# Batch 1's down products moved from fp32 parts to half-precision parts

## The chip, the cores and the metric

The kernel runs on one core of one Trainium2 chip. The core has five engines that run their own instruction streams: TensorE (PE in the profile, with its weight loads as PEld), VectorE (DVE), ScalarE (ACT), GpSimd (POOL) and SyncE (SP, here a queue of DMA issues). They wait for each other by semaphores. The metric is the device time of one execution in microseconds (us); less is better.

## The reference, cut to what matters

Four batches of 512 rows by 512 columns go through an attention-like block and then a feed-forward block with a residual sum each:

```python
x = x + _L0_attn_ref(_layernorm(x), W_q, W_kv, W_o)
x = x + _L0_ffn_ref(_layernorm(x), gate_w, up_w, down_w, gate_scale, up_scale, down_scale)

# attention: per head of 32 columns
qf  = l2_normalize(fft(q));  kvf = cumsum(l2_normalize(fft(kv)), axis=1)
out = ifft(qf * kvf).real @ W_o.T

# feed-forward, weights rounded to fp8, I = 1536
gate = silu((x @ gate_w8) * gate_scale)
up   = (x @ up_w8) * up_scale
y    = ((gate * up) @ down_w8) * down_scale
```

The change touches only the last product, `(gate * up) @ down_w8`, and what feeds it.

## The kernel before

**Tiling.** A batch `b` (0 to 3) has four row tiles `t` of 128 rows. The feed-forward has 12 slices `i` of 128 inner columns; a slice's number over all batches is `n = 12 * b + i`. TensorE makes for each slice a gate product in the PSUM bank `bg` and an up product in `bu` (`pe_gate_up`, 8 matmuls of 128x512 each), and a down product `pe_down` (8 matmuls: four row tiles `t`, each with a high and a low part, added up over the 12 slices in the banks `bd0` to `bd3`).

**Between them, for slice n:** ScalarE makes `sl` = silu(`bg`) (`act_silu`), VectorE makes `ff` = `bu` * scale * `sl` (`dve_f`), ScalarE copies `ff` into the high part (`act_fu`), and VectorE subtracts it for the low part (`dve_fu`). `pe_down(n)` needs both. `ff`, `fu` and `sl` have two buffers each, by `n % 2`.

**Two forms of the down product.** For `n < HALF * NI` the two parts and the weights (`fu`, `dw`) are 32-bit floats (fp32r). From `n = HALF * NI` on they are 16-bit floats (`fu16`, `dw16`), which the profile names by the memory they borrow, `half` and `own`. GpSimd copies the weights to 16 bits (`pool_dw`, six copies). With 16 bits `ff` could overflow, so it is divided by a power of two, the unit, which is worked out from the data and multiplied back in at the end (`us2` takes the place of the up scales `us`, `ds2` that of the down scales `ds`). `HALF` is 2 before: batches 0 and 1 have the 32-bit form, batches 2 and 3 the 16-bit one.

**The unit** comes from the largest absolute weight of each part of `gu` (`dve_most`, six reductions of 128x2048), a few tiny steps (`dve_gus`), one tiny matmul with ones that adds over the partitions (`pe_bound`, two passes of 128x3), and a chain of tiny steps on the result (before: `act_bound`, then `dve_unit2`).

**Order.** Every engine's order is written out by hand. After batch 0's own section a loop `for b in 1..3` runs; its turn `b` begins with `pe_qk` of the batch `nxt = b + 1` (7 products of 12 matmuls), then the first gate and up product of batch `b`, the last down product of batch `b - 1`, the eighth `pe_qk`, and so on. In the same turn VectorE sums squares for `nxt` (`dve_sum`, eight of them), scales batch `b - 1`'s finished banks by `ds` (`dve_scale_out`, into `ff`, so it takes turns with `dve_f`), and GpSimd adds that to `h` (`pool_out`). `dve_f(b * NI + 1)` writes the `ff` buffer that the third `pool_out` reads, and so waits for it. Then comes `dve_norm_tail` of `nxt` (a reciprocal and three short steps), `dve_scale(nxt, 0, 1)`, ScalarE's `act_ks`, GpSimd's `pool_ks`, and with these TensorE's `pe_tri(nxt, 0)`.

**PSUM banks.** `ba0` and `ba1` pass from piece to piece in the order of `tenancies()`; a piece waits until its bank's last tenant has been read.

## Time and profile before

| what | value |
|---|---|
| median of 3 runs | 419.12 us (418.77 to 419.37) |
| the profiled execution | 419.79 us, of which 418.0 us from its first to its last instruction |
| busy | PE 408.8 us (98%), DVE 297.4 (71%), ACT 193.2 (46%), POOL 108.2 (26%) |
| mean granted TensorE clock | 0.996 of full speed |

Times in rows are microseconds from the start of the span. TensorE overlaps one matmul with the next: a 128x512 matmul is listed with 379 ns, and in a row of them one starts every 216 ns. The chain of waits follows the work that ended last back in time and shows what each piece added to it.

### The profile page before, as it was taken

Reading aid. Unit: us, or ns where it says so; the run is one execution under the profiler, and the core shown is the slowest. Engines: PE = TensorE matmul, PEld = TensorE weight load, DVE = VectorE, ACT = ScalarE, POOL = GpSimd, SP = SyncE. Lnnn points to the kernel's source line nnn. Section 1 sums busy time; section 2 is a strip of 40 time slices with the busy share of each in tenths; the row PEclk is TensorE's granted clock in tenths of the full one; section 3 lists DMA queues with packets and bytes.
Section 4 is the critical chain, followed back from the end, with each engine's and each line's share of the span. In section 5 each row is a group of like instructions: output and inputs, shape, how many; then the busy total and the mean of one; then the engine's idle time right before and its main releaser. Section 6 shows DMA issues by size and latency. Waiting matters only on the chain.

```text
span 418.0 us, 5504 instructions
## 1 busy us (share of the span) xinstructions
PE 408.8 (98%) x1897; PEld 202.8 (49%) x1897; DVE 297.4 (71%) x514; ACT 193.2 (46%) x323; POOL 108.2 (26%) x114
## 2 busy tenths in 40 slices
PE   7999999999999999999999999999999999999994
PEld 3744454445555554454555555454444444444442
DVE  4998998999999699997984972167865854422234
ACT  3687756587736245445242563255442441131220
POOL 0133551015154137043541012032461001300003
PEclk9999999999999999999999999999999999999998
DMA  8986546600181143232112014411112051200002
GB/s 249 264 267 239 163 117 162 149 17 2 38 256 36 26 77 71 57 127 74 28 26 50 2 29 101 72 50 53 26 26 52 0 77 25 100 2 0 2 0 101
DMA packets 57547, 33.55 MB, mean 80 GB/s; under 512 B 49456, under 2 KB 49840, under 8 KB 57392
## 3 DMA queue, kind: packets, MB, share of 16 engines
q1 hardware_dynamic: 57088, 32.93, 30.3%
q8 instruction: 15, 0.25, 0.3%
q10 hardware_dynamic: 432, 0.28, 0.2%
q14 instruction: 12, 0.10, 0.1%
HBM read 17.44 MB, written 4.19 MB: 52 GB/s over the span
## 4 chain that ended last, share of the span: by engine, by line
PE 89%; DMA 3%; DVE 3%; ACT 2%; POOL 1%; SPq 1%; issue 1%; POOLq 0%; DVEq 0%
PE bd L488 20%; PE bu L470 19%; PE bg L470 19%; PE ba L370 14%; PE ba L415 8%; PE bd L370 3%; DMA h<-x_dram 1%; PE ba L388 1%; PE bd L415 1%; DMA hT<-w_q_dram 1%; PE bd L388 1%; PE bd L356 1%; PE bu L415 1%; POOL xs L1603 1%; PE bg L447 0%
## 5 line engine op out<-in xcount | busy, mean ns | idle before, releaser
L470 PE MATMUL bu<-hT,gu 128*128 128x512 f16 x384 | 90.7, 379 | 0.0
L470 PE MATMUL bg<-hT,gu 128*128 128x512 f16 x376 | 89.0, 379 | 0.0
L1234 DVE SCALAR_TENSOR_TENSOR ff<-bu,us,sl 128x512 f32<-128x512 f32 x48 | 35.9, 748 | 56.0 <-PE bu L470 52.8
L741 ACT ACTIVATE sl<-bg,gs 128x512 f32<-128x512 f32 x48 | 32.9, 686 | 78.0 <-PE bg L470 77.0
L370 PE MATMUL ba<-wf,xT 128*128 128x512 f16 x288 | 63.2, 379 | 0.0
L470 PEld LDWEIGHTS bu<-hT,gu 128*128 128x128 f16 x384 | 37.5, 98 | 45.5 <-DVE ff L1234 0.6
L470 PEld LDWEIGHTS bg<-hT,gu 128*128 128x128 f16 x376 | 35.6, 98 | 44.9 <-issue 4.1
L488 PE MATMUL bd<-dw,fu 128*128 128x512 f32 x192 | 51.1, 411 | 0.0
L1634 POOL TENSOR_TENSOR h<-ff,h 128x512 f32<-128x512 f32 x14 | 17.5, 1272 | 122.2 <-DVE ff L1265 122.2
L370 PEld LDWEIGHTS ba<-wf,xT 128*128 128x128 f16 x288 | 27.9, 98 | 34.1 <-issue 1.1
L488 PE MATMUL bd<-own,half 128*128 128x512 f16 x184 | 43.0, 379 | 0.0
L1603 POOL TENSOR_TENSOR xs<-xn,xs 128x512 f16<-128x512 f32 x15 | 20.4, 1369 | 79.7 <-ACT xs L653 79.7
L488 PEld LDWEIGHTS bd<-dw,fu 128*128 128x128 f32 x192 | 36.1, 188 | 9.6 <-DVE fu L1241 0.4
L1616 POOL TENSOR_TENSOR ks<-qk,ks 128x512 f16<-128x512 f32 x16 | 21.2, 1325 | 48.8 <-ACT ks L704 48.8
L415 PE MATMUL ba<-wo,qk 128*128 128x512 f16 x144 | 32.6, 379 | 0.0
L1050 DVE TENSOR_REDUCE S<-tu 128x16 f32<-128x512 f32 x32 | 21.5, 676 | 11.2 <-ACT tu L667 11.2
L488 PEld LDWEIGHTS bd<-own,half 128*128 128x128 f16 x184 | 17.9, 98 | 21.9 <-DVE half L1241 0.6
L1241 DVE TENSOR_TENSOR half<-ff,half 128x512 f16<-128x512 f32 x23 | 19.3, 839 | 11.9 <-ACT half L747 11.7
L667 ACT ACTIVATE tu<-ba 128x512 f32<-128x512 f32 x24 | 14.3, 594 | 22.2 <-PE ba L370 22.2
L1139 DVE TENSOR_TENSOR qk<-qk,sc 128x512 f32<-128x512 f32 x32 | 23.0, 736 | 0.2
L1241 DVE TENSOR_TENSOR fu<-ff,fu 128x512 fp32r<-128x512 f32 x24 | 20.8, 872 | 3.2 <-ACT fu L747 3.0
L747 ACT ACTIVATE half<-ff 128x512 f16<-128x512 f32 x23 | 14.3, 623 | 18.4 <-PE bd L488 13.2
(201 smaller groups left out, 524.3 us busy)
## 6 DMA issues: line engine op xcount, KB each, us to landing
h<-x_dram SPq DMA_DIRECT2D x16, 256.0 KB, 4.2
out_dram<-h SPq DMA_DIRECT2D x15, 256.0 KB, 2.0
hT<-w_q_dram SPq DMA_DIRECT2D x4, 256.0 KB, 5.0
gu<-w_kv_dram SPq DMA_DIRECT2D x4, 256.0 KB, 4.4
hT<-gate_w_dram SPq DMA_DIRECT2D x2, 512.0 KB, 3.5
hT<-up_w_dram SPq DMA_DIRECT2D x2, 512.0 KB, 5.6
gu<-woT_dram SPq DMA_DIRECT2D x1, 1024.0 KB, 5.1
hT<-down_w_dram SPq DMA_DIRECT2D x2, 512.0 KB, 4.9
```

The lines of the kernel that those rows point to most:

```text
L370: m = e.matmul(ba[i][:, :], xT[:, b % 2, part_x, k, P * t:P * t + P], wf[:, w, part_w, k, :], start=k == 0 and part_x == part_w, stop=k == ...
L415: m = e.matmul(ba[i][:, :], src[:, part_p, P * j:P * j + P], wo[:, part_w, j, :], start=j == 0 and part_p == part_w, stop=j == KT - 1 and ...
L470: m = e.matmul(bk[:, :], gu[:, c, 4 * w + k, col:col + P], hT[:, b % 2, part, k, :], start=k == 0 and part == 0, stop=k == KT - 1 and part ...
L488: m = e.matmul(bd[t][:, :], fu_at(n)[:, part, P * t:P * t + P], (dw if n < HALF * NI else dw16)[:, i, :], start=i == 0 and part == 0, stop ...
L741: e.activation(sl[:, n % 2, :], bg[:, :], ACT.Silu, scale=gs[:, i:i + 1]).then_inc(a_silu, 1)
L1050: e.tensor_reduce(S[:, t, NH * w:NH * w + NH], v, AX.X, ALU.add).then_inc(v_sum, 1)
L1139: e.tensor_tensor(split_heads(qk[:, t, w, :]), split_heads(qk[:, t, w, :]), head_scale(t, w), ALU.mult).then_inc(v_kn if w else v_qn, 1)
L1234: e.scalar_tensor_tensor(out=ff[:, n % 2, :], in0=bu[:, :], scalar=(us if b < HALF else us2)[:, i:i + 1], in1=sl[:, n % 2, :], op0=ALU.mul ...
L1241: e.tensor_tensor(fu_at(n)[:, 1, :], ff[:, n % 2, :], high.bitcast(F32) if n < HALF * NI else high, ALU.subtract).then_inc(v_fu, 1)
L1603: e.tensor_tensor(xs[:, t % 2, 1, :], xn[:, t % 2, :], xs[:, t % 2, 0, :], ALU.subtract).then_inc(p_xl, 1)
L1616: e.tensor_tensor(ks[:, 1, t, :], qk[:, t, 1, :], ks[:, 0, t, :], ALU.subtract).then_inc(p_ks, 1)
L1634: e.tensor_tensor(hh, y_at(b, t), hh, ALU.add).then_inc(p_out, 1)
```

## The change

`HALF` becomes 1: batch 1's 12 down products take the 16-bit form as well. Its first scaling by the unit is then in `dve_f(12)`, the first of turn `b = 1`, so the unit has to be ready there. For this:

- the first of the six `dve_most` moves from the start of turn 1 back into batch 0's section, ahead of `dve_f(10)`;
- `pe_bound` moves from behind the eighth `pe_qk` into the middle of `pe_down(11)`;
- the tiny steps behind it move from turn 1's middle (behind `dve_fu(15)`) ahead of `dve_f(12)`; ScalarE's step goes, and the steps are other ones (seven on VectorE where there were one on ScalarE and six on VectorE); the scaling of `ds` stays where it was;
- `dve_sum(nxt, 2, 1)` moves ahead of these steps, and `dve_sum(nxt, 3, 1)` ahead of `dve_scale_out(b - 1, 2)`, both in turn 1 only;
- in turn 1 ScalarE's high part waits also until the last weight has been rounded.

```diff
-HALF = 2
+HALF = 1
...
-        order += [("qk", b, t, w) for t in (1, 2, 3) for w in range(2)]
-        if b == HALF:
+        order += [("qk", b, t, w) for t in (1, 2) for w in range(2)] + [("qk", b, 3, 0)]
+        if b == HALF + 1:
             order += [("bound",)]
+        order += [("qk", b, 3, 1)]
...
                 pe_gate_up(e, b, 0)
-                pe_down(e, b * NI - 1)
+                pe_down_tile(e, b - 1, NI - 1, 0)
+                pe_down_tile(e, b - 1, NI - 1, 1)
+                if b == HALF:
+                    pe_bound(e)
+                pe_down_tile(e, b - 1, NI - 1, 2)
+                pe_down_tile(e, b - 1, NI - 1, 3)
                 if nxt < NB:
                     pe_qk(e, nxt, 3, 1)
-                if nxt == HALF:
-                    pe_bound(e)
...
-        def act_bound(e):
-            e.wait_ge(s_bound, 1)
-            e.activation(bound[:, 3:6], ba[AT["bound",]][:, 0:3], ACT.Sqrt).then_inc(a_bound, 1)
...
         def dve_unit2(e):
-            e.wait_ge(a_bound, 1)
-            e.tensor_tensor(bound[:, 9:10], bound[:, 3:4], bound[:, 4:5], ALU.mult).then_inc(v_unit2, 1)
+            e.wait_ge(s_bound, 1)
+            e.tensor_copy(bound[:, 3:6], ba[AT["bound",]][:, 0:3]).then_inc(v_unit2, 1)
             e.wait_ge(v_unit2, 1)
...
+            e.tensor_scalar(bound[:, 9:10], bound[:, 3:4], bound[:, 4:5], 1e-30, ALU.mult, ALU.max).then_inc(v_unit2, 1)
+            e.tensor_scalar(bound[:, 10:11], bound[:, 5:6], 1e-30, None, ALU.max).then_inc(v_unit2, 1)
...
+            e.reciprocal(bound[:, 14:15], bound[:, 13:14]).then_inc(v_unit2, 1)
+            e.wait_ge(v_unit2, 6)
+            e.tensor_scalar(us2[:, :], us[:, :], bound[:, 14:15], None, ALU.mult).then_inc(v_unit2, 1)
...
             if n == HALF * NI:
-                e.wait_ge(v_unit2, 6)
+                e.wait_ge(v_unit2, 7)
...
+            dve_most(e, 0, 0)
             dve_f(e, 10)
...
-                if nxt == HALF:
+                if b == HALF:
                     dve_most(e, 2, 0)
                     dve_most(e, 2, 1)
                     dve_gus(e)
+                    dve_sum(e, nxt, 2, 1)
+                    dve_unit2(e)
                 dve_f(e, b * NI)
                 dve_scale_out(e, b - 1, 0)
                 dve_fu(e, b * NI)
-                if nxt < NB:
+                if b > HALF and nxt < NB:
                     dve_sum(e, nxt, 2, 1)
                 dve_scale_out(e, b - 1, 1)
                 if nxt < NB:
                     dve_sum(e, nxt, 3, 0)
+                    if b == HALF:
+                        dve_sum(e, nxt, 3, 1)
                 dve_scale_out(e, b - 1, 2)
                 dve_scale_out(e, b - 1, 3)
...
-                if nxt == HALF:
-                    dve_unit2(e)
+                if b == HALF:
+                    dve_unit_out(e)
```

TensorE before, in turn 1 from the first gate and up product on (`bd` and `fu` is the down product `pe_down(11)`, `ba0<-wf,xT` the eighth `pe_qk`, `bound` the tiny matmul):

```order
L470 MATMUL bu<-hT,gu 128x512 [waits dve_f]
L470 MATMUL bu<-hT,gu 128x512 x7
L488 MATMUL bd0<-dw,fu 128x512 [waits dve_rd,dve_fu]
L488 MATMUL bd0<-dw,fu 128x512
L488 MATMUL bd1<-dw,fu 128x512 x2
L488 MATMUL bd2<-dw,fu 128x512 x2
L488 MATMUL bd3<-dw,fu 128x512 x2
L370 MATMUL ba0<-wf,xT 128x512 [waits d_xT3,act_cp]
L370 MATMUL ba0<-wf,xT 128x512 x11
L377 MATMUL ba1<-bound,ones 128x3 [waits dve_most,act_cp]
L470 MATMUL bg<-hT,gu 128x512 [waits act_silu]
```

The same place on TensorE in the changed kernel:

```order
L471 MATMUL bu<-hT,gu 128x512 [waits dve_f]
L471 MATMUL bu<-hT,gu 128x512 x7
L489 MATMUL bd0<-dw,fu 128x512 [waits dve_rd,dve_fu]
L489 MATMUL bd0<-dw,fu 128x512
L489 MATMUL bd1<-dw,fu 128x512 x2
L378 MATMUL ba0<-bound,ones 128x3 [waits dve_most,act_cp]
L489 MATMUL bd2<-dw,fu 128x512 x2
L489 MATMUL bd3<-dw,fu 128x512 x2
L371 MATMUL ba1<-wf,xT 128x512 [waits d_xT3,act_cp]
L371 MATMUL ba1<-wf,xT 128x512 x11
L471 MATMUL bg<-hT,gu 128x512 [waits act_silu]
```

The tiny matmul now stands between the second and the third row tile of `pe_down(11)`, and the two `ba` banks have changed places.

VectorE before, from the last tiny step of `dve_gus` to the reciprocal of `dve_norm_tail` (`ff<-bu` is `dve_f`, `ff<-bd` is `dve_scale_out`, `fu<-ff` is `dve_fu`, `S<-tu` is `dve_sum`):

```order
L1092 TENSOR_TENSOR bound<-bound 128x3 [waits dve_most]
L1234 SCALAR_TENSOR_TENSOR ff<-bu,us,sl 128x512 [waits dve_fu,act_silu,pe_u]
L1265 TENSOR_TENSOR ff<-bd0,ds 128x512 [waits dve_fu,pe_d]
L1241 TENSOR_TENSOR fu<-ff,fu 128x512 [waits act_fu]
L1050 TENSOR_REDUCE S<-tu 128x16 [waits act_sq]
L1265 TENSOR_TENSOR ff<-bd1,ds 128x512 [waits dve_fu,pe_d]
L1050 TENSOR_REDUCE S<-tu 128x16 [waits act_sq]
L1265 TENSOR_TENSOR ff<-bd2,ds 128x512 [waits pool_out,pe_d]
L1265 TENSOR_TENSOR ff<-bd3,ds 128x512 [waits pool_out,pe_d]
L1050 TENSOR_REDUCE S<-tu 128x16 [waits act_sq]
L1234 SCALAR_TENSOR_TENSOR ff<-bu,us,sl 128x512 [waits dve_fu,pool_out,act_silu,pe_u]
L1119 RECIPROCAL y0<-Q 128x128 [waits act_rt1]
```

VectorE in the changed kernel, from the sum and the tiny steps that now stand ahead of `dve_f(12)`:

```order
L1049 TENSOR_REDUCE S<-tu 128x16 [waits act_sq]
L1098 COPY bound<-ba0 128x3 [waits pe_bound]
L1100 TENSOR_SCALAR bound<-bound 128x1 [waits dve_unit2]
L1101 TENSOR_SCALAR bound<-bound 128x1
...
L1109 RECIPROCAL bound<-bound 128x1 [waits dve_unit2]
L1111 TENSOR_SCALAR us2<-us,bound 128x12 [waits dve_unit2]
L1238 SCALAR_TENSOR_TENSOR ff<-bu,us2,sl 128x512 [waits dve_fu,dve_unit2,act_silu,pe_u]
L1269 TENSOR_TENSOR ff<-bd0,ds 128x512 [waits dve_fu,pe_d]
L1245 TENSOR_TENSOR half<-ff,half 128x512 [waits act_fu]
L1269 TENSOR_TENSOR ff<-bd1,ds 128x512 [waits dve_fu,pe_d]
L1049 TENSOR_REDUCE S<-tu 128x16 [waits act_sq] x2
L1269 TENSOR_TENSOR ff<-bd2,ds 128x512 [waits pool_out,pe_d]
```

`dve_f(12)` now comes behind a wait for TensorE's tiny matmul and seven steps; one of the sums moved ahead of them, and another ahead of the third scaling.

## Rows read from the trace of the kernel before

**Rows 1.** By stretch: length, busy PE, PEld, DVE, ACT, POOL, granted clock, DMA share, GB/s.

```profile
156.00:253.00 97.00, 96.92 (x444) 50.80 (x443) 79.83 (x128) 46.64 (x74) 32.77 (x33) 1.00 0.21 52
...
412.00:418.00 6.00, 0.63 (x3) 0.10 (x1) 2.09 (x5) 0.00 (x0) 2.46 (x3) 0.75 0.47 175
```

**Rows 2.** The chain that ended last: start, us, what, in turns 1 and 2.

```profile
185.72 1.85 PE bd L488 x8
...
253.14 18.15 PE ba L370 x84
...
297.74 1.73 PE bd L488 x8
...
348.74 1.29 PE bg L470 x6
```

**Rows 3.** TensorE in order of time, turn 1, then turn 2's first `pe_tri`.

```profile
177.31 2.21 PE L488 MATMUL bd<-dw,fu 128*128 128x512 f32 x8
179.36 2.76 PE L370 MATMUL ba<-wf,xT 128*128 128x512 f16 x12
181.96 0.28 PE L377 MATMUL ba<-bound,ones 128*128 128x3 f32 x2
...
189.14 1.89 PE L470 MATMUL bu<-hT,gu 128*128 128x512 f16 x8
191.11 0.59 PE L388 MATMUL ba<-ks,tr 128*128 128x512 f16 x2
...
288.04 0.59 PE L388 MATMUL ba<-ks,tr 128*128 128x512 f16 x2 [0.21 <-POOL ks L1616]
```

**Rows 4.** VectorE in order of time, the start of turn 1.

```profile
178.18 0.75 DVE L1234 SCALAR_TENSOR_TENSOR ff<-bu,us,sl 128x512 f32<-128x512 f32 x1
...
179.62 1.80 DVE L1241 TENSOR_TENSOR fu<-ff,fu 128x512 fp32r<-128x512 f32 x1
...
182.54 0.67 DVE L1050 TENSOR_REDUCE S<-tu 128x16 f32<-128x512 f32 x1
183.13 0.68 DVE L1265 TENSOR_TENSOR ff<-bd,ds 128x512 f32<-128x512 f32 x1
184.06 0.69 DVE L1265 TENSOR_TENSOR ff<-bd,ds 128x512 f32<-128x512 f32 x1 [0.26 <-POOL h L1634]
...
185.76 0.75 DVE L1234 SCALAR_TENSOR_TENSOR ff<-bu,us,sl 128x512 f32<-128x512 f32 x1 [0.41 <-PE bu L470]
186.42 0.94 DVE L1119 RECIPROCAL y<-Q 128x128 f32<-128x128 f32 x1
```

**Rows 5.** GpSimd in order of time, the start of turn 1.

```profile
179.60 1.27 POOL L1634 TENSOR_TENSOR h<-ff,h 128x512 f32<-128x512 f32 x1 [11.88 <-DVE ff L1265]
182.69 3.75 POOL L1634 TENSOR_TENSOR h<-ff,h 128x512 f32<-128x512 f32 x3 [1.82 <-DVE ff L1265]
```

**Rows 6.** ScalarE in order of time, turn 1.

```profile
178.96 0.63 ACT L747 ACTIVATE fu<-ff 128x512 fp32r<-128x512 f32 x1 [0.35 <-DVE ff L1234]
...
184.73 1.28 ACT L680 ACT_TABLE_LOAD   x1
186.03 0.31 ACT L680 ACTIVATE Q<-S 128x128 f32<-128x128 f32 x1
```

**Rows 7.** VectorE, three of the unit's tiny steps in their old place.

```profile
206.02 1.09 DVE L1100 TENSOR_TENSOR bound<-bound 128x1 f32<-128x1 f32 x1
...
207.34 0.15 DVE L1104 TENSOR_SCALAR bound<-bound 128x1 int32<-128x1 int32 x1
207.53 0.16 DVE L1107 RECIPROCAL bound<-bound 128x1 f32<-128x1 f32 x1
```

**Rows 8.** VectorE, `dve_f(10)` with the idle time before it, and a `dve_most`.

```profile
143.81 0.75 DVE L1234 SCALAR_TENSOR_TENSOR ff<-bu,us,sl 128x512 f32<-128x512 f32 x1 [3.26 <-PE bu L470]
...
162.53 2.28 DVE L1081 TENSOR_REDUCE most<-gu 128x1 f32<-128x2048 f16 x1
```

**Rows 9.** TensorE's first matmuls of the program.

```profile
1.19 5.28 PE L338 MATMUL bd<-ks 128*128 128x512 f16 x14 [1.19 <-DVE ks L1029]
```

More of the change, by code:

```diff
@@ L197, in build @@
         a_zh, v_zl = sem("act_zh"), sem("dve_zl")
-        v_most, s_bound, a_bound, v_unit2, v_gus, p_dw = (
-            sem(n) for n in ("dve_most", "pe_bound", "act_bound", "dve_unit2", "dve_gus", "pool_dw"))
+        v_most, s_bound, v_unit2, v_gus, p_dw = (
+            sem(n) for n in ("dve_most", "pe_bound", "dve_unit2", "dve_gus", "pool_dw"))
         d_cst, d_cst2, d_id, d_wo, d_sc, d_carry = (sem("d_" + n) for n in ("cst", "cst2", "id", "wo", "sc", "carry"))
@@ L247, in emptied @@
             if kind == "bound":
-                return a_bound, 1
+                return v_unit2, 1
             if kind == "size":
@@ L746, in act_fu @@
                 e.wait_ge(s_d, 4 * (n - 1))
+            if n == HALF * NI:
+                e.wait_ge(*rounded(17))
             e.activation(fu_at(n)[:, 0, :], ff[:, n % 2, :], ACT.Copy).then_inc(a_fu, 1)
@@ L1252, in dve_scale_out @@
             if b == HALF and t == 0:
-                e.wait_ge(v_unit2, 7)
+                e.wait_ge(v_unit2, 8)
             if b < NB - 1:
@@ L1468, in vector_program @@
                     dve_sum(e, nxt, 0, 1)
[L1469 to L1470 removed]
+                if b == HALF:
+                    dve_most(e, 0, 1)
                 if nxt < NB:
                     dve_sum(e, nxt, 1, 0)
[L1473 to L1474 removed]
+                if b == HALF:
+                    dve_most(e, 1, 0)
                 if nxt < NB:
                     dve_sum(e, nxt, 1, 1)
[L1477 to L1478 removed]
+                if b == HALF:
+                    dve_most(e, 1, 1)
                 if nxt < NB:
                     dve_sum(e, nxt, 2, 0)
[L1481 to L1482 removed]
+                if b == HALF:
                     dve_most(e, 2, 0)
@@ L1493, in vector_program @@
                     dve_sum(e, nxt, 3, 0)
+                    if b == HALF:
+                        dve_sum(e, nxt, 3, 1)
                 dve_scale_out(e, b - 1, 2)
                 dve_scale_out(e, b - 1, 3)
-                if nxt < NB:
+                if b > HALF and nxt < NB:
                     dve_sum(e, nxt, 3, 1)
@@ L1673, in gpsimd_program @@
                 nxt = b + 1
-                if b + 1 == HALF:
+                if b == HALF:
                     for n in range(NI // 2):
```

28 lines of the change are left out of this document (8 added, 20 removed).

## The prediction

> **What bounds the kernel now.** I read the busy times by stretch first. In turn 1 TensorE is busy 96.92 of 97.00 us at full clock, while no other engine is busy for more than 80 [rows 1]. So a matmul that becomes shorter is worth its whole difference, and any new idle time of TensorE is lost. The chain of waits says the same: it runs over one TensorE group after the other [rows 2]. The one place in turn 1 where it leaves TensorE's own groups is the first `pe_tri`: the up product ahead of it starts at 189.14, its eight matmuls take 1.73 and end their turn at 190.87, and `pe_tri` starts at 191.11, some 0.24 later [rows 3]. What it waits for is the end of a chain over VectorE, ScalarE and GpSimd. The rest of the prediction is about whether that chain gets later, since the change adds work right ahead of it.
>
> **Part 1: the down products.** In the chain eight 32-bit matmuls take 1.85 us (185.72), eight 16-bit ones 1.73 (297.74) [rows 2]: 0.12 less. Twelve groups change, 12 x 0.12 = 1.44 us. A second way: from turn 1's first `pe_tri` to the next turn's first `pe_qk` it is 253.14 - 191.11 = 62.03 us; turn 2, whose ten down groups behind `pe_tri` have 16 bits already and whose other matmuls are the same, takes 348.74 - 288.04 = 60.70 [rows 2, 3]. That is 1.33 for ten groups and the small losses around them. One group, `pe_down(23)`, lies in turn 2 (0.13 by the same measure), and one, `pe_down(12)`, ahead of turn 1's `pe_tri`. So 1.33 + 0.13 = 1.46 us can be won behind `pe_tri`. What `pe_down(12)` gives, 0.12, only lets TensorE arrive earlier at a wait that exists already, and counts for nothing.
>
> **Part 2: when turn 1's first `pe_tri` can start.** Step by step from TensorE's tiny matmul:
>
> The tiny matmul now stands behind four of the eight matmuls of `pe_down(11)`. That group starts at 177.31, the next one at 179.36; four matmuls of 1.86 / 8 = 0.23 before the latter is 178.43, and the tiny one takes 0.28 [rows 3]: its result is there at 178.71, for VectorE at 178.75. What it is made of is ready before: the six reductions are five now, and end some 2.2 us earlier than before [rows 8], so that the sum that moved ahead fits in too.
>
> Then seven tiny steps. Two of them in a row that wait for each other start 0.19 apart (207.34, 207.53) [rows 7]; six such and one that waits for nothing (0.12, an estimate) are 1.26. Bounds: 0.12 each (0.8) if they overlap better, and for each that meets a GpSimd instruction up to 0.9 more, as the one at 206.02 with 1.09 instead of 0.15 [rows 7]. I take no meeting, because GpSimd then has nothing to do until the first scaling is done, and that comes behind these steps. So `dve_f(12)` starts at 180.02 instead of 178.18 [rows 4]: 1.84 later. No matmul waits for that itself: the up product that needs it starts near 183.8, and `dve_f(12)` ends at 180.8.
>
> From the start of `dve_f(12)` to the end of its `dve_fu` it was 181.42 - 178.18 = 3.24 [rows 4]; in that lies a stretch in which `dve_fu` stood still for GpSimd's first `pool_out` (179.60 to 180.87) and then took its last 0.55 [rows 4, 5]. I take the same: 183.26. After that `dve_scale_out` 1, two sums and `dve_scale_out` 2 follow. One of these starts 0.60 after the other (182.54, 183.13) and lasts 0.68 [rows 4]: the third scaling starts at 183.18 + 3 x 0.60 = 184.98 and ends at 185.66. Before, it ended at 183.81, with only one sum ahead of it instead of two; that is the other half of the delay.
>
> GpSimd's third addition starts 0.08 after that (as 179.60 after a scaling that ended at 179.52), takes 1.27 [rows 5] and ends at 187.01. Only then may `dve_f(13)` overwrite what it reads: 0.10 later (184.06 after an addition that ended at 183.96) [rows 4, 5], so at 187.11 instead of 185.76. Before, this wait was covered: the third addition ended near 185.2, and `dve_f(13)` waited for TensorE's up product until 185.76 [rows 4].
>
> `dve_norm_tail` stands behind `dve_f(13)` on VectorE and moves with it from 186.42 to 187.77. From there to `pe_tri` it is 191.11 - 186.42 = 4.69 [rows 3, 4], over a head scaling, ScalarE's `act_ks` and GpSimd's `pool_ks`, all of which have idle engines before them. `pe_tri` then starts at 192.46, **1.35 us later than before**. TensorE arrives at 190.75, or 0.1 later if the tiny matmul costs more between 32-bit weights, and stands for some 1.7 us.
>
> The next things that could be late instead are covered: `pe_down(12)` needs the fourth scaling at 186.86, which ends at 186.3; the up product of slice 14 needs `dve_f(13)`, done at 187.9, when it starts at 189.0. The moved reduction takes 2.28 us in an idle time of 3.26 ahead of `dve_f(10)` [rows 8]: nothing. The 16-bit weights are made by GpSimd at the same place as before, over ten microseconds ahead of `pe_down(12)`: nothing. The old tiny steps leave the middle of turn 1, where TensorE lost nothing to them: nothing.
>
> **The sum.** +1.35 (`pe_tri` later) - 1.33 (ten groups behind it) - 0.13 (`pe_down(23)`) = **-0.11 us**. The profiled execution took 419.79, so it would become 419.68; on the median of 419.12 it is **419.0 us**. Bounds from the tiny steps (0.8 to 1.26 + 0.9) and a half microsecond of either sign for the wake-ups that I took from neighbours give 418.4 to 420.0 for this case.
>
> **The rivals.**
>
> *The delay doesn't come about* (faster). ScalarE loads a table until 186.01 and takes the root until 186.34 [rows 6], and `dve_norm_tail` can't start before that. If `dve_f(13)` isn't held, `pe_tri` starts at 191.11 as before, and the kernel gains 1.46 us: 417.7. It needs the third addition to end by 185.8, 1.2 us earlier than I worked out. Against it speaks that each step is taken from a row; for it only that I could have misread which addition `dve_f(13)` waits for.
>
> *The other engine goes first* (faster). Before, GpSimd's first addition started at 179.60 and `dve_fu` at 179.62, and VectorE lost 1.1 us to the 0.02 [rows 4, 5]. If `dve_fu` started first, it would end at 182.2 and the addition would run from 182.2 to 183.5; the additions would follow each other without a gap, the third would end at 186.0, `dve_f(13)` would start at 186.1 and `dve_norm_tail` at 186.7, 0.3 later than before: 419.12 - 1.46 + 0.3 = 418.0. Against it: both starts hang on the same `dve_f(12)`, one over a scaling on VectorE and the other over ScalarE's copy, so their distance shouldn't change. The Trainium skill (page "SBUF — State Buffer", section "Who interferes with whom") states the rule for this: a VectorE instruction with two SBUF inputs and a GpSimd instruction that reads SBUF exclude each other for the whole instruction, and whichever was issued first goes first. By that rule, the trace agrees with its 1.80 us [rows 4], and 0.02 us decides over 1.1.
>
> *The standing TensorE loses its clock* (slower). The wait of 1.7 us in one piece is longer than any that TensorE has between its first and its last matmul. If its granted clock fell from 2.4 to 1.2 GHz on it, the price would be like that of the program's start, where 14 matmuls took 5.28 us instead of 14 x 0.216 = 3.02 [rows 9]: 2.3 us, so 421.3. It decides if the clock falls for more than 2 us. Against it: in the last stretch TensorE works 0.63 of 6 us and the mean clock is still 0.75, so it stood at full speed for about half of the idle time, some 3 us [rows 1].
>
> *More of the tiny steps meet GpSimd, or TensorE's tiny matmul waits* (slower, but little): each such costs up to 0.9, and it takes a whole further one to leave the band of 0.2%.
>
> **How the numbers follow.** My own case has a chance of 0.83 and gives 419.0. The delay that doesn't come about has 0.06 (417.7), the other engine first 0.05 (418.0), the clock 0.03 (421.3), a further meeting 0.03 (419.9 to 420.2). A measurement of this kernel can tell a difference of about 0.2%, 0.84 us, from none: faster means below 418.3, slower above 420.0. The two faster rivals make 0.11, and the lower edge of my own case 0.01 more: 0.12. Slower is the clock, half of the further meeting and a hundredth of my own case: 0.05. The rest, 0.83, is within 0.2%. The range goes from 417.9, which takes in the other-engine case, to 419.8, the upper end of my own case but for its last tenths.
>
> **What the profile of the changed kernel would show.** Right: the 96 down matmuls of slices 12 to 23 at 1.73 per group of eight; `dve_f(12)` starting about 1.8 us behind its old place relative to the first gate product of turn 1; `dve_f(13)` released by GpSimd's addition and no longer by TensorE's up product; before turn 1's first `pe_tri` about 1.7 us in which TensorE waits for `pool_ks`; from that `pe_tri` to the next turn 60.7 us. Wrong: if `dve_f(13)` is still released by the up product, or that wait is still 0.2 to 0.4 us, the kernel is more than a microsecond faster. If TensorE's matmuls behind the wait start 0.43 apart instead of 0.216, the clock has fallen. If new waits show up behind `pe_tri` in turn 1, the comparison with turn 2 was wrong, since turn 1 has batch 3's preparation to do beside it.

## The result: slower by 0.38%

| what | before | after |
|---|---|---|
| median of the comparison | 419.37 us (418.30 to 420.64, 19 executions) | 420.81 us (419.51 to 423.02, 19 executions) |
| ratio, with its 95% interval | 1 | 1.0038 (1.0024 to 1.0052) |
| the profiled execution | 419.79 us, span 418.0 | 420.53 us, span 418.7 |
| mean granted TensorE clock in it | 0.996 | 0.997 |

The prediction was 419.0, no measurable change, with a range up to 419.8. The kernel is slower by some 1.6 us by the ratio (1.44 between the two medians), beyond that range. The case of the largest chance was wrong, and so was the range.

TensorE in the changed kernel, in order of time (start, us, engine, line, operation, in brackets the idle time before it and its releaser); `half` and `own` are the 16-bit parts and weights. The last row counts 8 matmuls only because this view ends at 218; the group has 12:

```profile
178.04 0.28 PE L378 MATMUL ba<-bound,ones 128*128 128x3 f32 x2
...
185.25 1.89 PE L489 MATMUL bd<-own,half 128*128 128x512 f16 x8
...
188.70 1.89 PE L471 MATMUL bu<-hT,gu 128*128 128x512 f16 x8
192.56 0.59 PE L389 MATMUL ba<-ks,tr 128*128 128x512 f16 x2 [1.97 <-POOL ks L1624]
...
213.74 1.89 PE L471 MATMUL bu<-hT,gu 128*128 128x512 f16 x8
216.29 1.89 PE L416 MATMUL ba<-wo,qk 128*128 128x512 f16 x8 [0.66 <-DMA qk<-ks]
```

Here are both losses of this execution. Before the first `pe_tri` TensorE stands for 1.97 us, until `pool_ks` is done; reckoned as in [rows 3], from the point where the eight matmuls ahead of it (188.70) end their turn, that is 2.13 us against 0.24 before. And `pe_o(2, 1)` at 216.29 waits, which it did not do before. `pe_o(b, t)` is the product with the weights `wo` (the reference's `W_o`) for row tile `t` of batch `b`; its input `zT` is transposed by the DMA, into a buffer that the profile calls `qk`. The chain of waits (start, us, what) shows this second wait plainly. Before it stayed on TensorE:

```profile
212.95 1.73 PE bu L470 x8
214.68 1.35 PE ba L415 x6
```

After, it goes over SyncE's issue and the landing of `zT` for tile 1:

```profile
211.52 1.36 SPq L1736
212.88 0.04 issue
212.93 3.23 DMA qk<-ks
216.16 0.14 issue
216.29 0.81 PE ba L416 x3
```

VectorE after, the counterpart of [rows 4]:

```profile
178.36 0.16 DVE L1098 COPY bound<-ba 128x3 f32<-128x3 f32 x1 [0.88 <-PE ba L378]
178.55 0.21 DVE L1100 TENSOR_SCALAR bound<-bound 128x1 f32<-128x1 f32 x1
...
179.52 0.23 DVE L1111 TENSOR_SCALAR us<-us,bound 128x12 f32<-128x12 f32 x1
179.90 0.75 DVE L1238 SCALAR_TENSOR_TENSOR ff<-bu,us,sl 128x512 f32<-128x512 f32 x1
...
181.34 1.80 DVE L1245 TENSOR_TENSOR half<-ff,half 128x512 f16<-128x512 f32 x1
183.25 0.69 DVE L1269 TENSOR_TENSOR ff<-bd,ds 128x512 f32<-128x512 f32 x1
...
187.21 0.75 DVE L1238 SCALAR_TENSOR_TENSOR ff<-bu,us,sl 128x512 f32<-128x512 f32 x1 [0.89 <-POOL h L1642]
187.88 0.94 DVE L1123 RECIPROCAL y<-Q 128x128 f32<-128x128 f32 x1
```

And GpSimd, the counterpart of [rows 5]:

```profile
181.32 1.27 POOL L1642 TENSOR_TENSOR h<-ff,h 128x512 f32<-128x512 f32 x1 [13.98 <-DVE ff L1269]
184.01 1.27 POOL L1642 TENSOR_TENSOR h<-ff,h 128x512 f32<-128x512 f32 x1 [1.42 <-DVE ff L1269]
185.80 2.49 POOL L1642 TENSOR_TENSOR h<-ff,h 128x512 f32<-128x512 f32 x2 [0.52 <-DVE ff L1269]
```

This is the mechanism of the prediction: `dve_f(13)` (187.21) is now released by GpSimd's third addition (`h`) and no longer by TensorE's up product, and everything behind it is late.

A third loss is in none of these lines, since this execution didn't have it. Of the 19 executions of the changed kernel, 8 have a mean granted clock of 0.995 or less, with a median of 421.95 us; the other 11 have 420.34. The section on the clock below shows what these are.

**A yardstick for the experiments.** TensorE's times ahead of turn 1 scatter by about a microsecond from execution to execution, in the kernel before too (turn 1's first `pe_qk` starts at 155.91 in one profile of it and at 157.18 in another). So I compare turn 1 alone: from its first `pe_qk` to turn 2's first. Two profiles of the kernel before give 97.07 and 97.02, two of the changed kernel 98.37 and 98.48. From there to the end it is 164.99 and 164.99 before, 164.84 and 164.83 after.

### The profile page after: what moved, and what is told of

It is laid out like the page before. It is cut to its first block, busy times and chain, and to the rows that moved or that the text cites. A ratio compares the mean times of both kernels' runs of the same rounds, so it can differ in the third digit from the quotient of the medians.

```text
span 418.7 us, 5504 instructions
## 1 busy us (share of the span) xinstructions
PE 407.7 (97%) x1897; PEld 195.2 (47%) x1897; DVE 298.0 (71%) x515; ACT 193.4 (46%) x322; POOL 108.4 (26%) x114
## 4 chain that ended last, share of the span: by engine, by line
PE 83%; DVE 5%; DMA 3%; POOL 3%; ACT 3%; issue 1%; SPq 1%; POOLq 0%; DVEq 0%; ACTq 0%
PE bg L471 17%; PE bu L471 17%; PE bd L489 17%; PE ba L371 13%; PE ba L416 7%; PE bd L371 3%; PE bd L339 2%; DMA h<-x_dram 1%; PE ba L389 1%; PE bd L416 1%; POOL ks L1624 1%; DMA qk<-qk 1%; DMA qk<-ks 1%; PE bd L389 1%; PE bd L357 1%
## 5 line engine op out<-in xcount | busy, mean ns | idle before, releaser
L489 PE MATMUL bd<-own,half 128*128 128x512 f16 x280 | 65.4, 379 | 0.0
L489 PEld LDWEIGHTS bd<-own,half 128*128 128x128 f16 x280 | 27.2, 98 | 33.3 <-DVE half L1245 0.9
L1245 DVE TENSOR_TENSOR half<-ff,half 128x512 f16<-128x512 f32 x35 | 30.5, 873 | 14.5 <-ACT half L749 14.2
L749 ACT ACTIVATE half<-ff 128x512 f16<-128x512 f32 x35 | 21.8, 623 | 22.3 <-PE bd L489 14.1
L489 PE MATMUL bd<-dw,fu 128*128 128x512 f32 x96 | 25.8, 412 | 0.0
L416 PEld LDWEIGHTS ba<-wo,qk 128*128 128x128 f16 x144 | 13.9, 98 | 18.0 <-issue 2.0
L1633 POOL TENSOR_TENSOR qk<-tu 128x256 f32<-128x256 f32 x14 | 12.2, 870 | 32.8 <-DVE tu L1166 32.8
```

Source lines behind the costliest of these rows:

```text
L416: m = e.matmul(ba[i][:, :], src[:, part_p, P * j:P * j + P], wo[:, part_w, j, :], start=j == 0 and part_p == part_w, stop=j == KT - 1 and ...
L489: m = e.matmul(bd[t][:, :], fu_at(n)[:, part, P * t:P * t + P], (dw if n < HALF * NI else dw16)[:, i, :], start=i == 0 and part == 0, stop ...
L749: e.activation(fu_at(n)[:, 0, :], ff[:, n % 2, :], ACT.Copy).then_inc(a_fu, 1)
L1245: e.tensor_tensor(fu_at(n)[:, 1, :], ff[:, n % 2, :], high.bitcast(F32) if n < HALF * NI else high, ALU.subtract).then_inc(v_fu, 1)
```

## The experiments

All ratios are to the kernel before, measured beside the kernel in question, with their 95% interval. "Turn 1" and the waits are from one profiled execution each. "Wait" is how much later than its pace TensorE starts that product, so it is a few hundredths to 0.2 us more than the idle time in brackets in a row.

| kernel | ratio | turn 1, us | wait ahead of `pe_tri(2,0)` | wait ahead of `pe_o(2,1)` | executions at a clock of 0.995 or less |
|---|---|---|---|---|---|
| before, again | 0.9999 (0.9985 to 1.0013) | 97.02 | 0.24 | under 0.12 | 0 of 12 |
| changed, again | 1.0054 (1.0037 to 1.0070) | 98.48 | 2.12 | 0.94 | 2 of 6 |
| early unit, 32 bits | 1.0086 (1.0065 to 1.0107) | 99.49 | 2.01 | 0.66 | 2 of 6 |
| known unit | 0.9980 (0.9966 to 0.9994) | 96.32 | 0.38 | 0.52 | 0 of 10 |
| own third | 1.0021 (1.0011 to 1.0030) | 97.64 | 1.43 | 0.80 | 0 of 12 |
| other order | 0.9988 (0.9975 to 1.0002) | 97.04 | 0.82 | 0.80 | 0 of 11 |
| 16 waits | 1.0048 (1.0028 to 1.0068) | 100.37 | 2.13 | 0.16 | 7 of 12 |
| other order, 16 waits | 0.9999 (0.9987 to 1.0011) | 97.15 | 0.81 | 0.16 | 0 of 12 |
| filled wait | 1.0031 (1.0017 to 1.0045) | 98.75 | 0.74 | 0.95 | 0 of 12 |
| one ScalarE instruction | 1.0028 (1.0012 to 1.0044) | 99.49 | 2.12 | 0.17 | 3 of 12 |
| other order, late addition | 1.0015 (1.0001 to 1.0029) | 97.73 | 0.38 | 1.03 | 0 of 12 |
| the same, one ScalarE instruction | 0.9987 (0.9976 to 0.9997) | 97.04 | 0.38 | 0.27 | 0 of 12 |
| other order, one ScalarE instruction | 0.9983 (0.9970 to 0.9996) | 96.47 | 0.80 | 0.21 | 0 of 11 |

The profiled executions of "16 waits" and "one ScalarE instruction" are among those at the lower clock, so their turn 1 contains some 1.7 us that the others don't have.

### Is it the unit's place, and not the 16 bits?

Both kernels once more, for the scatter:

> The kernel before once more, for a second profile of it. Theory A: TensorE again waits under 0.15 us ahead of pe_o(2, 1) and 0.24 us ahead of turn 1's first pe_tri; what differs from the first profile lies ahead of 150 us, in the wait for rounded weights near 99 us. Rival (the 0.8 us ahead of pe_o(2, 1) come and go with the execution): half a microsecond or more also stands there in this profile.

> The changed kernel once more, unchanged, for a second profile. Theory A (a wait that is always there): turn 1's first pe_tri again waits about 2.1 us for GpSimd, and 1.0 to 1.4 us over the kernel before is the typical result. Theory B (something that comes and goes with the execution, such as the 0.8 us that TensorE waited for the transposed tile of pe_o(2, 1) while two instruction-fetch packets of 8 KB took 0.78 us each, or a spell of low clock behind the long wait): the first profile's 0.8 us is gone or stands elsewhere, and the total moves by about 1 us with it, or matmuls 0.43 us apart show up inside the span.

Measured: 0.9999 and 1.0054. The result stands, and both waits come again in the changed kernel's second profile (2.12 and 0.94) and neither in that of the kernel before. The two packets that the expectation puts at 0.78 us each took 0.33 and 1.23 in the first profile. The lower clock doesn't explain why the changed kernel's ratio is higher the second time (1.0054, 1.0038 before): only 2 of these 6 executions have it, and the other 4 have a median of 421.24 us, where the first 11 had 420.34. The intervals overlap, and the difference stays open.

The early unit alone, with the down products left at 32 bits:

```diff
-HALF = 1
+HALF = 2
+UNIT = 1
...
-                if b == HALF:
+                if b == UNIT:
                     dve_most(e, 2, 0)
```

> The unit is worked out at the new, early place and dve_f(12) waits for it, but batch 1 keeps its 32-bit down products. Theory A (the early unit holds turn 1's first pe_tri by 1.84 us, and this is paid whole): 1.8 us slower than the kernel before, ratio 1.0043. Rival (the wait costs less, since a later wait takes it up, and the half-precision parts themselves are what costs): less than 0.8 us slower.

The 16 bits alone, with the unit taken out of the way:

```diff
+KNOWN = 1.0
...
             if n == HALF * NI:
-                e.wait_ge(v_unit2, 7)
+                e.wait_ge(v_known, 1)
...
+            e.tensor_scalar(us2[:, :], us[:, :], 1.0 / KNOWN, None, ALU.mult).then_inc(v_known, 1)
             dve_f(e, 10)
```

> Batch 1 in half-precision parts as in the changed kernel, but the unit is taken as known (1.0): dve_f(12) waits for nothing, all reductions, the tiny matmul and the tiny steps are still made, the steps behind dve_fu(15) as before, and nobody uses their result. Theory A: the whole gain of 1.46 us of the twelve groups less what is left of waits, 1.2 to 1.5 us faster than the kernel before, ratio 0.9965 to 0.9971. Rival (the half-precision form brings losses of its own): no faster than before.

Measured: 1.0086 for the first and 0.9980 for the second. The first is above its expectation, which knew neither of the wait at `pe_o` nor of the clock; its profile has 2.4 of the 3.6 us in turn 1, where the rest of these six executions comes from stays open. The second gains 0.8 us and not the 1.2 to 1.5 expected. TensorE in these two, at its first `pe_tri` of turn 1:

```profile
193.12 0.59 PE L390 MATMUL ba<-ks,tr 128*128 128x512 f16 x2 [1.85 <-POOL ks L1625]
```

```profile
192.11 0.59 PE L391 MATMUL ba<-ks,tr 128*128 128x512 f16 x2 [0.22 <-POOL ks L1631]
...
215.55 2.75 PE L418 MATMUL ba<-wo,qk 128*128 128x512 f16 x12 [0.36 <-DMA qk<-ks]
```

So the long wait comes with the unit's early place, whatever the form of the down products. Turn 1 takes 99.49 with the early unit alone and 98.37 to 98.48 with both. The two waits of the table are together 0.28 to 0.39 shorter in the former, so the eleven groups of 16 bits in turn 1 give 1.4 us (the middle of the difference, 1.06, and of the waits, 0.34), which is 0.13 each. With the 16 bits alone turn 1 takes 96.32. The 16 bits do what they were to do, and the loss is all in the rest. But the known unit still left 0.52 ahead of `pe_o(2,1)`, which neither of my theories had.

### Where does the chain to `pe_tri` lose its time?

The third scaling into a buffer that is unused at that time (`pT`, declared as plain 32-bit floats for this), so that `dve_f(13)` doesn't wait for the third addition; the scaling's own wait for an addition goes with it:

```diff
         def y_at(b, t):
...
-            return ff[:, (t + 1) % 2, :]
+            return pT[:, 0, :] if (b, t) == (0, 2) else ff[:, (t + 1) % 2, :]
...
-                e.wait_ge(p_out, 4 * (b - 1) + 2 + i)
+                e.wait_ge(p_out, 1 if n == NI + 1 else 4 * (b - 1) + 2 + i)
```

> The changed kernel, but batch 0's third scaling goes into a buffer of its own, so that dve_f(13) does not wait for GpSimd's third addition. Theory A (that addition holds dve_f(13)): dve_f(13) starts right behind the fourth scaling, 1.0 us earlier than in the changed kernel, turn 1's first pe_tri too, and the kernel is 0.9 to 1.0 us faster than the changed one, about 0.4 us or less slower than the kernel before or equal. Rival (the delay comes from VectorE's own queue, the addition only ends last): less than 0.3 us faster than the changed kernel.

Measured: `dve_f(13)` starts without a wait as expected, but the wait ahead of `pe_tri` shrinks by 0.7 only. VectorE of this kernel, with GpSimd's fourth addition beside it, and `pe_tri`:

```profile
186.78 0.74 DVE L1238 SCALAR_TENSOR_TENSOR ff<-bu,us,sl 128x512 f32<-128x512 f32 x1
...
188.42 0.57 DVE L1125 SCALAR_TENSOR_TENSOR Q<-y 128x128 f32<-128x128 f32 x1
```

```profile
187.58 1.26 POOL L1644 TENSOR_TENSOR h<-ff,h 128x512 f32<-128x512 f32 x1
```

```profile
192.41 0.59 PE L389 MATMUL ba<-ks,tr 128*128 128x512 f16 x2 [1.27 <-POOL ks L1626]
```

A step of `dve_norm_tail` takes 0.57 instead of 0.29 us: it ended 188.99, right behind the addition (188.84). What was won in the buffer was partly lost to the neighbour.

Both the third and the fourth scaling in buffers of their own, and a sum instead of a scaling ahead of `dve_fu(12)`:

```diff
...
                 dve_f(e, b * NI)
-                dve_scale_out(e, b - 1, 0)
+                if b == HALF:
+                    dve_sum(e, nxt, 3, 0)
+                else:
+                    dve_scale_out(e, b - 1, 0)
                 dve_fu(e, b * NI)
+                if b == HALF:
+                    dve_scale_out(e, b - 1, 0)
...
```

> The changed kernel with VectorE's order behind dve_f(12) turned round: dve_sum(2, 3, 0) and dve_fu(12) first, then all four scalings, the third and fourth into buffers of their own, then the last sum. GpSimd has then nothing to do while dve_fu(12) runs, and dve_f(13) waits for the first addition only. Theory A (the chain from dve_f(12) to dve_f(13) is what the early unit costs): dve_fu(12) takes 0.7 us, dve_f(13) is released by TensorE again, turn 1's first pe_tri waits 0.4 us or less, and the kernel is 1.7 us faster than the changed one and 0.5 to 0.9 us faster than the one before (0.8 us ahead of pe_o(2, 1) stay). Rival (something else is late by then, such as the fourth scaling for pe_down(12)): a wait of TensorE of its own, and no faster than the kernel before.

Measured: a ratio of 0.9988 where the changed kernel had 1.0038 and 1.0054. `dve_fu(12)` no longer meets an addition (0.69 instead of 1.80), `dve_f(13)` is again released by TensorE, and the wait is 0.82. It is not below 0.4, since the same step of `dve_norm_tail` met the fourth addition again, and longer. VectorE and GpSimd:

```profile
181.41 0.69 DVE L1245 TENSOR_TENSOR half<-ff,half 128x512 f16<-128x512 f32 x1
...
185.52 0.75 DVE L1238 SCALAR_TENSOR_TENSOR ff<-bu,us,sl 128x512 f32<-128x512 f32 x1 [0.43 <-PE bu L471]
...
187.16 0.73 DVE L1125 SCALAR_TENSOR_TENSOR Q<-y 128x128 f32<-128x128 f32 x1
```

```profile
185.24 2.50 POOL L1647 TENSOR_TENSOR h<-pT,h 128x512 f32<-128x512 f32 x2
```

Moving that addition behind `pool_ks(2, 0)`:

```diff
-                pool_out(e, b - 1, 3)
+                if b != HALF:
+                    pool_out(e, b - 1, 3)
                 if nxt < NB:
                     pool_ks(e, nxt, 0)
+                    if b == HALF:
+                        pool_out(e, b - 1, 3)
```

> The kernel with own buffers and the other order of VectorE's steps (order_own), and GpSimd's fourth addition of turn 1 moved behind pool_ks(2,0). There the second step of dve_norm_tail took 0.73 instead of 0.29 us, as it had to wait for that addition. Theory: the step takes 0.29 again, pe_tri waits 0.4 us instead of 0.8, and 0.4 us are won: a ratio of 0.998 to the kernel before, where order_own had 0.9988. Rival: the addition, now near 191 us, holds VectorE's next product, dve_f(14) and what hangs on it, and pe_tri(2,1) starts as much later as was won: 0.9988 or more.

Measured: 1.0015. The rival was right, and the loss is larger than what was won. VectorE, GpSimd and TensorE of this kernel:

```profile
187.89 0.29 DVE L1125 SCALAR_TENSOR_TENSOR Q<-y 128x128 f32<-128x128 f32 x1
...
191.92 2.36 DVE L1143 TENSOR_TENSOR qk<-qk,sc 128x512 f32<-128x512 f32 x2
```

```profile
191.41 1.72 POOL L1647 TENSOR_TENSOR h<-pT,h 128x512 f32<-128x512 f32 x1
```

```profile
191.60 0.59 PE L389 MATMUL ba<-ks,tr 128*128 128x512 f16 x2 [0.22 <-POOL ks L1629]
...
201.59 0.59 PE L389 MATMUL ba<-ks,tr 128*128 128x512 f16 x2 [0.73 <-POOL ks L1629]
```

The step takes 0.29 and `pe_tri(2,0)` starts 0.44 earlier relative to its turn. But two products of VectorE take 2.36 instead of 1.28 us beside the moved addition, and the next `pe_tri` waits 0.89 us, where it had no wait above 0.12 in the other order. That is 0.45 more than was won, and the wait ahead of `pe_o(2,1)` is 1.03 instead of 0.80: turn 1 is 0.69 us longer. The collision was moved to a worse place.

### What delays `pe_o(2,1)`?

In the DMA's records two packets of 8 KB of the queue that the profile calls "instruction" fall into the transposition of `zT` for tile 1, which `pe_o` waits for. The DMA view of the changed kernel from 213.0 to 213.6 (queue: packets, MB, share; then the issue and its median time to landing):

```profile
q14 instruction: 2, 0.02, 16.3%
...
qk<-ks SPq DMA_TRANSPOSE x1, 3.2
```

The kernel before, from 212.2 to 213.0; its other fetch is at 206.16:

```profile
q14 instruction: 1, 0.01, 2.4%
...
qk<-ks SPq DMA_TRANSPOSE x1, 2.6
```

One fetch alone took 0.31 us there; of the two together, at 213.17 and 213.39, the second took 1.23 us. Which engine's code a packet holds isn't in these records; I call a fetch by the engine whose instruction count moves it, below. First I tried to move VectorE's, by 16 pairs of waits that are long satisfied ("16 waits" in the table):

```diff
+                if b == HALF:
+                    for _ in range(PAD):
+                        e.wait_ge(v_zero, 1)
+                        e.wait_ge(v_one, 1)
                 dve_f(e, b * NI + 3)
```

> The changed kernel with 16 waits that are already satisfied on VectorE, in its idle time ahead of dve_f(15). They cost nothing there, and move VectorE's later instructions on by 16 places, 1 KB of code. Theory C (in the changed kernel two instruction fetches of 8 KB, one of them VectorE's, now fall together into the transfer that pe_o(2, 1) waits for): VectorE's fetch comes some 5 to 8 us earlier, alone, the wait ahead of pe_o(2, 1) falls from 0.8 to 0.94 us to under 0.3, and the kernel is 0.5 to 0.8 us faster than the changed one. Rival (the transfer is late because VectorE and GpSimd are, the fetches only happen to be there): the fetches part, the wait stays at 0.6 or more.

> The turned order and the 16 waits together. Theories A and C: both waits are down, turn 1's first pe_tri at 0.4 us, pe_o(2, 1) under 0.3, and the kernel is 1.3 to 1.5 us faster than the one before, ratio 0.9965 to 0.997. Rival: as for the two parts, no faster than the turned order alone.

Measured: 1.0048 and 0.9999, no gain in either. The first has 7 of 12 executions at the lower clock, but it gains nothing without them either: the other five have a median 1.0 us above the kernel before, and the changed kernel's 11 such executions were 0.97 above. The fetches moved (to 205.14 and 216.53 in the one, 203.28 and 213.29 in the other), and the wait ahead of `pe_o` fell from 0.8 to 0.16 in both. But the fetch near 204 now fell beside a small DMA (2 KB, `qk<-qk`, the carried row of the running sum), which landed after 2.4 and 2.7 us instead of 1.7; GpSimd waited 4.67 us for it instead of 3.36 (the other order, with and without the 16 waits). That the fetch delayed it is likely, but no run separates the two. Behind it an up product of TensorE waits, 0.79 us in the one kernel and 0.57 in the other. Here that of the former:

```profile
216.73 1.90 PE L472 MATMUL bu<-hT,gu 128*128 128x512 f16 x8 [0.63 <-DVE ff L1239]
```

So this experiment shows that the instruction count moves a fetch and takes away the wait at `pe_o`, but not what the wait is worth. ScalarE is the cleaner handle: the change took one instruction from it, `act_bound`. So one is put back at the same place:

```diff
                     act_sqrt1(e, nxt, range(NT))
+                    if b == HALF:
+                        e.activation(bound[:, 15:16], us[:, 0:1], ACT.Sqrt)
                     act_ks(e, nxt, 0)
```

> The changed kernel with one further ScalarE instruction, a square root of 128x1 into an unused column, where act_bound stood before (between act_sqrt1 and act_ks in turn 1; ScalarE has over 3 us of idle time there). ScalarE's stream then has as many instructions ahead of turn 1's middle as in the kernel before. Theory A (ScalarE's next block of code is fetched at a place that one instruction shifts, and two fetches together in the middle of the transposition of zT for tile 1 delay pe_o): the two 8 KB fetches lie apart again, one near 207 to 208 us and one near 213, the time from the end of zl(2,1) to pe_o falls from 4.8 - 4.9 to 4.2, TensorE's wait ahead of pe_o from 0.8 - 0.9 to 0.1 - 0.2, and the kernel gains 0.6 to 0.7 us against the changed one. Theory B (the wait ahead of pe_o comes from the later start of the chain ahead of it): the fetches may move, the wait stays at 0.8. The 2.1 us wait ahead of pe_tri stays under both, and with it the executions of a low clock.

Measured: the fetches lie at 209.28 and 215.10, apart as before the change. The DMA view from 209.0 to 209.9 and from 214.8 to 215.8, with a landing of 2.9 us (the median of two transpositions) in the latter:

```profile
q14 instruction: 1, 0.01, 2.5%
```

```profile
q14 instruction: 1, 0.01, 3.2%
...
qk<-ks SPq DMA_TRANSPOSE x2, 2.9
```

The wait ahead of `pe_o` is 0.17 instead of 0.82 to 0.94, and the chain stays on TensorE there. The ratio is 1.0028, against 1.0038 and 1.0054 for the changed kernel: in the direction expected, but the intervals overlap, and this kernel too has executions at the lower clock. Its other nine have a median 0.89 us above the kernel before, the changed kernel's were 0.97 and 1.98 above. So the times don't fix what the wait is worth; the 0.6 to 0.8 us are from the profiles. What decides on the cause is the profiles too, in three pairs that differ by this one instruction: the wait ahead of `pe_o` goes from 0.82 and 0.94 to 0.17, from 0.80 to 0.21, and from 1.03 to 0.27.

### Does the wait cost the clock?

In the profile of the kernel with one further ScalarE instruction, TensorE's clock fell behind the wait, which ended at 193.04. The stretch that contains the wait, the next one and the one after that, then the same stretch behind the wait in the changed kernel's profile (length, busy PE, PEld, DVE, ACT, POOL, granted clock, DMA share, GB/s):

```profile
190.50:193.50 3.00, 1.04 (x6) 0.22 (x4) 2.57 (x5) 2.44 (x4) 1.15 (x1) 1.00 0.75 248
193.50:196.90 3.40, 3.40 (x10) 1.26 (x10) 3.06 (x6) 1.27 (x2) 0.26 (x1) 0.54 0.02 4
196.90:205.00 8.10, 8.10 (x38) 3.67 (x37) 4.42 (x6) 3.99 (x7) 3.75 (x5) 0.98 0.00 0
```

```profile
193.00:196.40 3.40, 3.40 (x17) 1.58 (x17) 3.08 (x6) 1.28 (x3) 0.24 (x1) 1.00 0.05 15
```

Ten matmuls instead of 17 in the same time: most of them start 0.43 apart instead of 0.216, that is at 1.2 instead of 2.4 GHz. From this `pe_tri` to the next it is 10.79 us instead of 9.10, so the lower clock costs 1.7. The first eight matmuls behind `pe_tri` are one row:

```profile
193.50 3.34 PE L489 MATMUL bd<-own,half 128*128 128x512 f16 x8
```

The kernel with 16 waits shows the same (clock 0.50 in the same stretch); its turn 1 is longer by that. To tell whether the pause is the cause, it was filled:

```diff
             vacant(e, ("tri", b, t))
+            if (b, t) == (HALF + 1, 0):
+                for k in range(FILL):
+                    e.matmul(ba[i][:, :], gu[:, 0, k % KT, 0:P], hT[:, 1, 0, k % KT, :], start=True, stop=True)
             e.wait_ge(p_ks, 4 * b + t + 1)
```

> The changed kernel, with six further matmuls of 128x512 ahead of turn 1's first pe_tri. They stand before its wait for pool_ks, multiply things that are long there, and write the bank that pe_tri then overwrites; nothing else is changed. TensorE reaches this place about 2.1 us before pool_ks is done, so six matmuls (6 x 0.216 = 1.3 us) lie inside the wait: pe_tri starts where it did, and TensorE stands for 0.8 us instead of 2.1. Theory A (the long wait costs TensorE its clock in part of the executions): in the kernels that waited 2.0 us or more here 17 of 43 executions had a mean granted clock of 0.995 or less and took some 1.6 us longer, in those that waited 1.4 us or less none of 167. Here then none has it, and the median falls to that of the others, about 0.7 us below the changed kernel's: a ratio to the kernel before of 1.002 to 1.003. Theory B (the low clock has another cause, such as the chip at that moment): again some 4 in 10 executions have it, and the ratio stays at 1.0038 to 1.0054.

(The counts in that text are off: it was 19 of 43 executions with the long wait, and none of 113 in the kernels with the shorter one and in the kernels before measured beside them.)

Measured: none of 12, and a ratio of 1.0031, whose interval overlaps the changed kernel's. TensorE in it, the six further matmuls and the two waits:

```profile
191.21 1.46 PE L387 MATMUL ba<-hT,gu 128*128 128x512 f16 x6
193.24 0.60 PE L393 MATMUL ba<-ks,tr 128*128 128x512 f16 x2 [0.57 <-POOL ks L1628]
...
217.47 2.75 PE L420 MATMUL ba<-wo,qk 128*128 128x512 f16 x12 [0.79 <-DMA qk<-ks]
```

`pe_tri` starts where it did (36.94 us behind the turn's start, 37.04 in the changed kernel), so nothing but the pause has changed there. Over all runs, the kernels with a wait of 2.0 to 2.1 us have 22 of 55 executions with a mean clock of 0.995 or less. Those with a wait of 1.43 or less have none of 210, the kernel before and these 12 included. If filling did nothing, 12 executions without one would come up in 0.6 to the 12th, 2 in 1000; by the share of the unfilled kernel measured beside it (one ScalarE instruction, 3 of 12) it is 3 in 100. Theory A stands, on the counts and not on the ratio.

### Do the repairs add up?

> late_add and the one ScalarE instruction together. If the wait ahead of pe_o is due to the two fetches and the one ahead of pe_tri to the addition, both go: 0.4 and 0.6 to 0.7 us less than order_own, a ratio to the kernel before of 0.996 to 0.9965, some 1.6 us faster than it. What is left of the gain of the 16-bit products (1.6 us) is then not lost anywhere. If either theory is wrong the ratio is 0.998 (only the addition) or 0.9975 (only the fetches).

> The kernel with own buffers and the other order of VectorE's steps (order_own) and the one further ScalarE instruction, without the late addition, since that gave 0.44 us ahead of pe_tri(2,0) and took 0.5 to 0.6 us ahead of pe_tri(2,1). If the two waits are independent, pe_tri(2,0) waits 0.8 us as in order_own, pe_tri(2,1) less than 0.4, pe_o(2,1) 0.2 instead of 0.8: 0.6 us less than order_own, a ratio to the kernel before of 0.997 to 0.9975, some 1.1 us faster. If the fetches only shifted the loss, as with the 16 further VectorE waits, the ratio stays at 0.9987 or above.

Measured: 0.9987 (0.9976 to 0.9997) and 0.9983 (0.9970 to 0.9996). The first misses its expectation of 0.996, since the late addition gives nothing (above). The second is the fastest kernel of the study that works the unit out from the data, 418.72 against 419.73 us for the kernel before measured beside it, and faster than both kernels, though by less than the 0.997 to 0.9975 that I expected. Its TensorE:

```profile
191.61 0.59 PE L389 MATMUL ba<-ks,tr 128*128 128x512 f16 x2 [0.64 <-POOL ks L1631]
...
214.74 2.75 PE L416 MATMUL ba<-wo,qk 128*128 128x512 f16 x12
```

Turn 1 takes 96.47, that is 0.57 less than in the kernel with the other order alone (97.04), as expected from the fetches. With the last part's 0.15 the profiles say 0.7 us faster than before, or 0.9983. Of the 1.46 us that the 16-bit products can give behind `pe_tri`, half comes through. Most of the rest is the wait of 0.8 ahead of `pe_tri`, of which 0.24 was there before.

## Why the prediction was wrong

**Right: part 1, the down products.** A group of eight takes 1.73 us instead of 1.85. Behind turn 1 the kernel became 0.15 us shorter (0.13 predicted), and early unit against changed kernel gives 1.4 us in turn 1 for eleven groups.

**Right: the mechanism of part 2.** `dve_f(13)` is released by the third addition, `pe_tri` by `pool_ks`, and both rivals on the faster side fell: `dve_f(13)` was held, and GpSimd's first addition again started 0.02 us ahead of `dve_fu(12)` (181.32, 181.34). The single steps, each against the changed kernel's own start of the turn (0.40 earlier than before):

| step | predicted | measured |
|---|---|---|
| copy of the tiny matmul's result | 178.75 - 0.40 = 178.35 | 178.36 |
| from there to `dve_f(12)` | 1.27 | 1.54 |
| `dve_f(12)` to the end of `dve_fu(12)` | 3.24 | 3.24 |
| from there to the end of the third addition | 3.75 | 3.92 |
| from there to `dve_f(13)` | 0.10 | 0.14 |
| `dve_f(13)` to `pe_tri` | 5.35 | 5.35 |
| `pe_tri` later than before by | 1.35 | 1.84 |

**Wrong, a size: the tiny steps.** I took 0.19 for each, and the first ones keep to it (178.36, 178.55). The last one, which scales the 12 columns, and `dve_f(12)`, which reads its result, lie 0.38 apart (179.52, 179.90), and the steps ahead of and behind the reciprocal are 0.25 and 0.20 from it. That is 0.27 in sum. The other 0.21 is for the most part that the second scaling waits for `dve_fu(12)` to end (183.25) where I had let it start before. Together 0.48 of the miss.

**Wrong, a step: "The old tiny steps leave the middle of turn 1, where TensorE lost nothing to them: nothing."** They cost no time there, but their removal, of the ScalarE step above all, moved where ScalarE's code is fetched (from 206.16 to 213.2), into the same fraction of a microsecond as VectorE's and into a transposition whose landing TensorE had no time to spare for. With one ScalarE instruction put back the wait was gone. From `pe_tri` to the next turn I expected 1.33 less and it became 0.54 less (61.33 against 61.87 from matmul to matmul). That is 0.79 of the miss, and I had priced it at nothing, without a bound.

**Wrong, a chance: the clock.** I gave 0.03 to the case that the standing TensorE loses its clock, and argued from the stretch at the kernel's end, where the mean clock over 6 us with 0.63 us of work was still 0.75 [rows 1]. That row says what one pause at one moment did. It doesn't say what a pause does in other executions. The case isn't all or nothing: it happens in 4 of 10 executions and then costs 1.6 to 1.7 us (I had priced it at 2.3), which moves the changed kernel's median by some 0.5 us (420.81 with these executions, 420.34 without). I also put the wait at 1.7 us; it became 2.1, and the runs show none with a lower clock at 1.43 and two fifths at 2.0 to 2.1. What 1.7 us would have done is open.

**The sum again.** 1.84 - 0.54 - 0.15 = 1.15 us for the profiled execution without the clock's loss, and with its start 0.40 earlier 0.75, as the spans have it (418.0, 418.7). With 0.5 for the clock it is 1.65, as the 1.6 measured. The -0.11 missed by 0.48, 0.79 and 0.5. That it comes out so closely is in part luck, with executions that scatter by a microsecond ahead of turn 1.

**The range** was too narrow even by its own terms: the bounds that I named (0.46 less or 0.9 more for the tiny steps, 0.5 of either sign) add up to 418.0 to 420.4, not to 418.4 to 420.0. It held neither of the two losses that I had put at nothing or nearly so.

**Of "what would show it wrong"** I had named the matmuls 0.43 apart and new waits behind `pe_tri` in turn 1. Both came. Having written them down as possible, I should have let the range reach them.

## What to carry to other kernels

A step that is late by a microsecond on a path with no slack doesn't only cost that microsecond: the pause that it makes can take TensorE's clock with it, in part of the executions, so a wait that goes from 0.2 to 2 us should be priced with both and the range should reach the larger one. When a change makes an engine that never waited stand still, look at whether matmuls can be put into the pause; here six useless ones took that loss away. And once TensorE has no slack, even a removed instruction on an idle engine can add a wait of 0.7 us, so compare the DMA's instruction packets of the two kernels at each transposition before you explain a new wait by the change's own logic.
